# Feed-forward rotation: sine products on ScalarE tile by tile, output stores elsewhere; attention: V products of two key tiles in a row

## What is computed

```
x   = ln(src) * (1 + scale) + shift          # scale, shift from the step's embedding
q, k, v = x Wq + bq, x Wk + bk, x Wv + bv
p   = softmax(q k^T / sqrt(32) + attention_bias, masked)
x   = x + (p v) Wo + bo
h   = ln(x) * g2 + beta2
y   = x + gelu2(h W1 + b1) W2 + b2           # gelu2(u) = u * sigmoid(1.702 u)
# rotation, for each group of four columns of y, angles theta, phi of the batch
out = (y0 ct + y1 st, -y0 st + y1 ct, y2 cp + y3 sp, -y2 sp + y3 cp)
```

## Time and profile before

| | |
|---|---|
| median of 3 runs | 3400.22 us (3399.85 to 3401.56) |
| the profiled execution | 3405.53 us, its span 3403.7 us |
| PE busy | 3227.8 us (95%) |
| POOL busy | 2219.2 us (65%) |
| DVE busy | 2162.2 us (64%) |
| ACT busy | 1758.6 us (52%) |
| granted TensorE clock, mean | 0.986 |

### The profile page before, as it was taken

One profiled execution on the slowest core, in us unless ns is written; L12 is line 12 of the kernel. 1 busy time (PEld: TensorE's weight loads), 2 busy tenths in 40 slices (PEclk: granted clock), 3 DMA queues, 4 the chain that ended last, 5 costly groups with the idle time before them and its releaser, 6 DMA issues.

```text
span 3403.7 us, 52439 instructions
## 1 busy us (share of the span) xinstructions
PE 3227.8 (95%) x16592; PEld 2377.2 (70%) x16592; DVE 2162.2 (64%) x4445; ACT 1758.6 (52%) x3785; POOL 2219.2 (65%) x1503
## 2 busy tenths in 40 slices
PE   5999999999999999999969999999999999999997
PEld 4676776766776776776547677686877768677685
DVE  3777777777777777777667554545545455454542
ACT  2777777777777777777734232332323323232331
POOL 3788888888887888887546653555445454553525
PEclk9999999999999999999989999999999999999998
DMA  5998998989899988898666576574757658576563
GB/s 187 257 271 254 254 272 263 264 255 260 252 271 263 266 266 254 257 266 251 194 208 247 189 249 202 196 252 161 247 182 241 210 168 258 168 249 202 180 204 136
DMA packets 440432, 785.15 MB, mean 231 GB/s; under 512 B 57024, under 2 KB 106176, under 8 KB 440160
## 3 DMA queue, kind: packets, MB, share of 16 engines
q1 hardware_dynamic: 440160, 781.82, 75.1%
HBM read 591.76 MB, written 89.19 MB: 200 GB/s over the span
## 4 chain that ended last, share of the span: by engine, by line
PE 43%; DMA 2%; issue 2%; DVE 1%; POOL 1%; SPq 1%; ACT 0%; POOLq 0%; DVEq 0%; ACTq 0%
PE ps_out L1394 19%; PE ps_first L1374 18%; PE ps_first L1415 6%; DMA w_ring<-w_parts 2%; PE ps_first L1427 1%; DVE w_ring L1733 1%; POOL turned_out L1654 0%; DMA tmp<-context_t 0%; DVE turned_out L1773 0%; POOL turned_out L1653 0%; ACT g_hi L1491 0%; POOL y_b L1641 0%; SPq L1163 0%; DMA turned_out<-in_L_cond_W_dram 0%; DVE h_lo L1795 0%
## 5 line engine op out<-in xcount | busy, mean ns | idle before, releaser
L676 POOL TENSOR_TENSOR biasm<-biasm,maskb 128x1024 f32<-128x1024 f32 x512 | 1091.5, 2148 | 255.6 <-DMA biasm<-in_fside_Bx16xSxS_dram 252.7
L1394 PE MATMUL ps_out<-w_ring,g_hi 128*128 128x512 f32 x2048 | 691.4, 403 | 52.9 <-issue 39.2
L1374 PE MATMUL ps_first<-h_hi,w_ring 128*128 128x512 f32 x1792 | 558.9, 393 | 18.5 <-DVE tmp L1846 10.1
L1593 POOL TENSOR_TENSOR g_lo<-g_now,g_hi 128x512 fp32r<-128x512 f32 x128 | 168.4, 1316 | 539.0 <-ACT g_hi L1491 539.0
L1394 PEld LDWEIGHTS ps_out<-w_ring,g_hi 128*128 128x128 f32 x2048 | 391.2, 191 | 154.0 <-issue 67.4
L783 PE MATMUL ps_score<-k_rows,q_rows 96*128 96x512 f32 x1024 | 494.7, 483 | 3.6 <-issue 3.3
L923 DVE CUSTOM_DVE_ANT_0 prob_first<-ps_score,biasm 128x512 f32<-128x512 f32 x512 | 347.2, 686 | 214.1 <-PE ps_score L783 175.1
L834 ACT ACTIVATE probT<-ps_probT 128x512 f32<-128x512 f32 x512 | 304.6, 595 | 255.3 <-PE ps_probT L796 251.1
L923 DVE CUSTOM_DVE_ANT_0 prob_last<-ps_score,biasm 128x512 f32<-128x512 f32 x512 | 346.8, 686 | 122.7 <-PE ps_score L783 111.7
L850 ACT ACTIVATE prob_first<-prob_first,negmax 128x512 f32<-128x512 f32 x512 | 365.2, 716 | 91.0 <-DVE negmax L923 90.0
L796 PE MATMUL ps_probT<-ident,prob_first 128*128 128x128 f32 x2048 | 393.0, 273 | 16.3 <-DVE probT L501 13.7
(11 more groups left out here) (159 smaller groups left out, 5650.0 us busy)
## 6 DMA issues: line engine op xcount, KB each, us to landing
biasm<-in_fside_Bx16xSxS_dram SPq DMA_DIRECT2D x512, 512.0 KB, 5.4
w_ring<-w_parts SPq DMA_DIRECT2D x240, 512.0 KB, 3.6
w_ring<-w_parts SPq DMA_DIRECT2D x392, 256.0 KB, 3.5
k_rows<-k_hi SPq DMA_DIRECT2D x512, 64.0 KB, 4.8
q_rows<-q_hi SPq DMA_DIRECT2D x512, 64.0 KB, 3.3
xn<-in_x_dram SPq DMA_DIRECT2D x16, 1024.0 KB, 7.1
normal_rows<-xn SPq DMA_DIRECT2D x16, 1024.0 KB, 7.7
k_rows<-k_lo SPq DMA_DIRECT2D x256, 64.0 KB, 4.5
```

The costliest lines, as they stand in the source:

```text
L676: pool.tensor_tensor(tile, tile, maskb[:, 2 * half:2 * half + 2, :], ALU.add).then_inc(masked.sem, 1)
L1374: mm = pe.matmul(ps[:, BANK[n], :], w1r[:, place, w, cols], h[:, n, c, :], start=(c == 0 and k == 0 and not onto), stop=(c == 1 and k == 2 ...
L1394: mm = pe.matmul(ps_out[:, t, :], a[:, k % 2, cols], w2r[:, k % VR, w, :], start=(m == 0 and n == 0), stop=(m == NF - 1 and n == 2))
L1593: pool.tensor_tensor(GLO[:, k % 2, :], src, GHI[:, k % 2, :].bitcast(F32), ALU.subtract).then_inc(glo_done.sem, 1)
```

## The change

- Attention: V products of key tiles i and i + 1 both stand in the even slot i of the group's first head; the odd slots have none. The waits of each key tile come with it.
- `cross` moves from GpSimd to ACT, with `activation(Copy, scale=column)` in place of `tensor_scalar`. For e = 0 it stands behind `split_g` 4, 5, 8 and 9, one tile each; for e = 1 in steps 1 to 4 of the next pair, behind the last tanh and ahead of `split_g`. At the end of the run four in a row.
- `store_out` of e = 0 moves to m = 4, 5, 8 and 9 in SP's queue, one each, and `load_ysum` from m = 6 to m = 9. For e = 1 `rotate` and `store_out` come one step later (steps 2 to 5), `load_ysum` in step 6.
- The four totals of e = 1 move from between `u2` and `u3` of step 0 to behind the last gelu of that step. The list of rotations of e = 0 on DVE is written in another way and gives the same order.

```diff
--- before.py
+++ after.py
@@ -751,20 +751,18 @@
                 for j, i in slots(mode):
                     g, h = j // GH, j % GH
                     before = group_before(mode, b, g)
-                    if before is not None and h == 0:
-
-
+                    for kt in ((i, i + 1) if before is not None and h == 0 and i % 2 == 0 else ()):
                         pb, pg = before
-                        ((outT_act if i % 2 == 0 else outT_dve)
-                         .wait(pe, pb, 2 * (GH * pg + GH - 1) + i // 2))
+                        ((outT_act if kt % 2 == 0 else outT_dve)
+                         .wait(pe, pb, 2 * (GH * pg + GH - 1) + kt // 2))
                         if pg == 0:
-                            v_done.wait(pe, *v_event(pb, i))
-                        if i == 0:
+                            v_done.wait(pe, *v_event(pb, kt))
+                        if kt == 0:
                             ctx_done.wait(pe, b - 1 if g == 0 else b, NG - 1 if g == 0 else g - 1)
                         for hh in range(GH):
                             head = GH * pg + hh
-                            mm = pe.matmul(ps_ctx[HD * hh:HD * (hh + 1), 0, :], V[:, (NT * pb + i) % VR, HD * head:HD * (head + 1)],
-                                           probT[:, hh, i, :], start=(i == 0), stop=(i == NT - 1),
+                            mm = pe.matmul(ps_ctx[HD * hh:HD * (hh + 1), 0, :], V[:, (NT * pb + kt) % VR, HD * head:HD * (head + 1)],
+                                           probT[:, hh, kt, :], start=(kt == 0), stop=(kt == NT - 1),
                                            skip_group_check=True)
                         mm.then_inc(pv_done.sem, 1)
                     t = score_tile(mode, b, j, i)
@@ -1286,9 +1284,9 @@
                         load_rows(p + 1, 0)
                         for t in range(NT):
                             load_ctx(p + 1, 0, t)
-                    if 1 <= s <= NT and p > 0:
-                        store_out(p - 1, 1, s - 1)
-                    if s == NT + 1 and p > 0:
+                    if 2 <= s <= NT + 1 and p > 0:
+                        store_out(p - 1, 1, s - 2)
+                    if s == NT + 2 and p > 0:
                         load_ysum(p, 0)
                     if s == (NT if p else NT + 1) and ahead:
                         load_rows(p + 1, 1)
@@ -1318,11 +1316,14 @@
                     if ahead and m in (1, 2):
                         store_y(p + 1, NT + 2 * (m - 1))
                         store_y(p + 1, NT + 2 * (m - 1) + 1)
-                    if m in (4, 5):
-                        store_out(p, 0, 2 * (m - 4))
-                        store_out(p, 0, 2 * (m - 4) + 1)
-                    if m == 6:
-                        load_ysum(p, 1)
+                    if m in (4, 5, 8):
+                        store_out(p, 0, (4, 5, 8).index(m))
+                    if m == 9:
+                        finish_first(p)
+
+            def finish_first(p):
+                store_out(p, 0, NT - 1)
+                load_ysum(p, 1)
 
             start()
             for p in range(NP):
@@ -1525,6 +1526,19 @@
                     t_done.wait(act, q, T_OF[k - 6])
                 act.activation(HH[:, n, c, :], hf_of(e, cc), ACT.Copy).then_inc(hh_done.sem, 1)
 
+            def cross(p, e, t):
+                b = 2 * p + e
+                sum_done.wait(act, p, NT * e + t)
+                j = NT * e + t
+                out_done[t % 2].wait(act, p if j >= 2 else p - 1, j // 2 - 1 if j >= 2 else NT - 1)
+                rotated.wait(act, p if j >= 2 else p - 1, j - 2 if j >= 2 else 2 * NT - 2 + j)
+                y = ysum[:, t, :].rearrange("p (q r) -> p q r", r=4)
+                o = turned_out[:, t % 2, :, :]
+                for n in range(2):
+                    act.activation(o[:, :, 2 * n], y[:, :, 2 * n + 1], ACT.Copy, scale=rot[:, n, b:b + 1])
+                    mm = act.activation(o[:, :, 2 * n + 1], y[:, :, 2 * n], ACT.Copy, scale=rot[:, 4 + n, b:b + 1])
+                mm.then_inc(crossed.sem, 1)
+
             for e in range(2):
                 for i in range(NC):
                     take_columns(0, e, i)
@@ -1565,9 +1579,13 @@
                     tanh(p, s, 1, I_U3)
                     tanh(p, s, 2, I_C21)
                     tanh(p, s, 3, I_C12)
+                    if p > 0 and 1 <= s <= NT:
+                        cross(p - 1, 1, s - 1)
                     split_g(p, 0, 2 * s + 1)
                 for m in range(NF):
                     split_g(p, 1, m)
+                    if m in (4, 5, 8, 9):
+                        cross(p, 0, (4, 5, 8, 9).index(m))
                     if ahead and m in (5, 6):
                         take_columns(p + 1, 0, 2 * (m - 5))
                         take_columns(p + 1, 0, 2 * (m - 5) + 1)
@@ -1583,6 +1601,8 @@
                     if ahead and m in (11, 12, 13, 14):
                         split_columns(p + 1, 6 + 2 * (m - 11))
                         split_columns(p + 1, 7 + 2 * (m - 11))
+            for t in range(NT):
+                cross(NP - 1, 1, t)
 
         @block.gpsimd
         def _(pool):
@@ -1640,20 +1660,6 @@
                         pool.wait_ge(y_out[j % 2], y_out_at(q, j) - 16)
                 pool.tensor_tensor(to, yr[:, e, t, :], b2_rows[:, :], ALU.add).then_inc(y2_done.sem, 1)
 
-            def cross(p, e, t):
-                b = 2 * p + e
-                sum_done.wait(pool, p, NT * e + t)
-                j = NT * e + t
-                out_done[t % 2].wait(pool, p if j >= 2 else p - 1, j // 2 - 1 if j >= 2 else NT - 1)
-                rotated.wait(pool, p if j >= 2 else p - 1, j - 2 if j >= 2 else 2 * NT - 2 + j)
-                y = ysum[:, t, :].rearrange("p (q r) -> p q r", r=4)
-                o = turned_out[:, t % 2, :, :]
-                pool.sem_inc(pool_waited, 1)
-                for n in range(2):
-                    pool.tensor_scalar(o[:, :, 2 * n], y[:, :, 2 * n + 1], rot[:, n, b:b + 1], None, ALU.mult)
-                    mm = pool.tensor_scalar(o[:, :, 2 * n + 1], y[:, :, 2 * n], rot[:, 4 + n, b:b + 1], None, ALU.mult)
-                mm.then_inc(crossed.sem, 1)
-
             for j in range(NT):
                 modulate(0, j)
             power(0, 0)
@@ -1666,8 +1672,6 @@
             for p in range(NP):
                 ahead = p + 1 < NP
                 for s in range(NS):
-                    if p > 0 and 1 <= s <= NT:
-                        cross(p - 1, 1, s - 1)
                     if p == 0 and s + 1 < NS:
                         if s == 0:
 
@@ -1693,16 +1697,11 @@
                     power(p + 1, 3)
                 for m in range(2, NF):
                     split_g(p, 1, m)
-                    if m in (5, 7):
-                        cross(p, 0, m - 5)
-                        cross(p, 0, m - 4)
                     if ahead and m == 2:
                         power(p + 1, NT)
                         power(p + 1, NT + 1)
                     if ahead and m in (3, 4):
                         power(p + 1, NT + m - 1)
-            for t in range(NT):
-                cross(NP - 1, 1, t)
 
         @block.vector
         def _(dve):
@@ -1825,9 +1824,6 @@
                     dve.tensor_tensor(tmp[:, I_U2, :], ps[:, Y, :], tmp[:, I_P1, :], ALU.add).then_inc(u2_done.sem, 1)
                     if p == 0 and s + 1 < NS:
                         make_w1(s + 1, range(3))
-                    if p > 0 and s == 0:
-                        for t in range(NT):
-                            total(p - 1, 1, t)
                     prod.wait(dve, p, NW * s + N_S3)
                     u2_done.wait(dve, p, s)
                     if s == 0:
@@ -1838,8 +1834,8 @@
                     gelu(p, s, 0, I_C11)
                     if p == 0 and s + 1 < NS:
                         make_w1(s + 1, range(3, NW))
-                    if p > 0 and 1 <= s <= NT:
-                        rotate(p - 1, 1, s - 1)
+                    if p > 0 and 2 <= s <= NT + 1:
+                        rotate(p - 1, 1, s - 2)
                     f = s + NS
                     prod.wait(dve, p, NW * s + N_S1)
                     u3_done.wait(dve, p, s)
@@ -1854,6 +1850,9 @@
                         .then_inc(c12_done.sem, 1)
                     gelu(p, s, 2, I_C21)
                     gelu(p, s, 3, I_C12)
+                    if p > 0 and s == 0:
+                        for t in range(NT):
+                            total(p - 1, 1, t)
                 if ahead:
                     add(p + 1, 0)
                     add(p + 1, 1)
@@ -1875,11 +1874,12 @@
                     add(p + 1, NT + 3)
                     normalize(p + 1, NT + 2)
                     normalize(p + 1, NT + 3)
-                for t in range(NT):
+                for t in range(NT - 1):
                     rotate(p, 0, t)
                     if ahead and t == 1:
                         for k in range(4):
                             split_columns(p + 1, k)
```

(1 more changed line is left out.)

## The result

The changed kernel takes 3345.63 us (median of 4 runs, 3340.82 to 3351.45) against 3400.89 of the kernel before: ratio 0.9834, interval 0.9821 to 0.9846, some 55 us less. Forecast were 3327 and 73 us less. Time lies in the range (3300 to 3357), the direction is right, and the gain is three quarters of what was worked out.

A forecast was written before the change was run, and what follows sets the result against it. TensorE was taken as the bound in attention; in feed-forward second halves it waited for GpSimd's g_lo and others. 23.3 + 7 x 6.0 - 2.1 - 5.6 + 10.1 + 5.0 = 72.7 us saved: forecast 3327, range 3300 to 3357.

The forecast's parts named there:

- Price of a V product: Attention on TensorE: 1.19 us alone, of which 0.335 for leaving and entering; pairing saves 0.67 per group of four.
- Slot 32: Attention: the second V pair delays the transpose of x and its chain by 0.5 us, 7.5 us lost over 15 batches.
- Slots 0, 16 and 48: Attention: V groups there are followed by work that waits for nothing, so 46 groups save 0.67 each, 30.8 us.
- The clock: Feed-forward pairs: the one long wait before m = 12 may bring half clock; 0.8 us a pair, 5.6 lost.
- Cross on ACT: Feed-forward: four operations of 0.31 us, 1.25 a tile, fit ACT's queue under a limit of 1.97 without TensorE waiting.
- The tail: End of the run, after TensorE: faster cross lets the last rotation start earlier, 5.0 us gained.
- GpSimd's two waits: Second half of a pair, before m = 6 and 8: TensorE's waits for g_lo go, 6.0 us gained per pair.
- the wait before m = 12: Second half of a pair: ACT's split_g stands behind a split awaiting DVE's combine; about 3 us remain in one piece.
- The last pair: Its twelve products from 3331.98: 10.1 us of waits for cross and for loads behind stores, all gained.
- SP: Feed-forward: moved stores free the w2 loads and remove the load wait at m = 11; nothing counted for it.
- Late loads: Rival, attention: full DMA engines make mask additions wait for bias loads, the 30.8 us are lost: 3358; chance 0.16.
- The strided rival: Rival, feed-forward: ACT's strided cross costs what GpSimd's does, 2.9 us a tile, 22 us in all: 3352; chance 0.10.

The follow-up runs named there:

- single products: The changed kernel with the four V products at slots 32 to 35 one per slot again, other groups in pairs: 3333.6 us, ratio 0.9791.
- the stores alone: The kernel before with only the four stores and the ysum load of the second half at their new places in SP's queue: 3412.4 us, ratio 1.0026.

## Why the prediction was right, and where it was wrong

- **Price of a V product: right.** 1.86 for a pair (1.85 forecast); 0.59 and 0.65 per group against 0.67.
- **Slot 32: right.** -0.54 against -0.5, by the place named, and undone by single products.
- **Slots 0, 16 and 48 "are followed by work that waits for nothing": the step that failed.** It holds for two. The group at slot 48 gave 0.13, not 0.67, 14 x 0.54 = 7.6 of the 12 us missed in attention: four slots shorter by 0.67 left DVE, with the statistics of x in its queue, no room for its copy (with the statistics behind slot 52 the wait is gone). I had read DVE's mean share (153 of 200 us) where its queue in those slots was needed. In the one batch without statistics the interval is 24.48, the whole 0.67.
- **The clock: near in size by luck, wrong in place.** 5.6 were set for the seven pairs; two fell, 4.5, and in the other traces with the same wait none or one. That the clock "did not fall" behind the wait at m = 8 holds for the pair that was read, and not for the one at 2780. But in attention, where I had none, it fell in three batches, 4.2 us, behind the grown wait that I had forecast ("grown to about 2"; it is 0.58 and 1.27) without asking what it does to the clock.
- **Cross on ACT: mechanism right, size off.** 1.67 for 1.25, since the step of four costs 0.12 an operation; under the limit, so no wait. The tail gave 4.7 for 5.0.
- **GpSimd's two waits, the wait before m = 12, the totals: right.** 5.9 a pair for 6.0 less 0.3; 2.77 for about 3; 0.21 for 0.3. But DVE's chain alone was not what held m = 12: with ACT's splits one product later the wait is 0.83, before m = 13.
- **The last pair: right in size, misread.** 10.1 for 10.1, but the prediction called all of it waits; 6.4 were, and the clock and the new starts made the rest.
- **SP: right** that clearing its queue is worth nothing. The fall of the clock behind the merged wait, which the prediction did count (0.8 a pair), makes it a loss where the GpSimd waits stay; my 3400 for the stores alone had left it out.
- **Rivals.** Late loads did not decide this kernel, but batches made long by waits for transfers go from none to two a trace to five or six once attention is another 0.5 us a batch faster. The strided rival of 2.9 a tile is out at 1.67; its price was, if anything, low, as 2.4 a tile already cost 23 us.
- **From the profiled run to the median.** 5.3 us taken off that the changed kernel's own profiled run did not have; with runs up to 11 us apart in the changed kernel and 14 in the one before, that step adds its own error.

## What to carry to other kernels

Read the other engines' queues in the very slots that get shorter, not their mean share: a group whose successor waits for nothing today may wait for a copy once four slots are 0.67 us shorter. Before removing a wait or merging several, look at what the clock does behind waits of that length; a long one in one piece can cost more than two short ones (205.2 us a pair against 203.7). And put an operation that waits behind, not ahead of, the one that the bound engine needs next: moving eight such operations gave 23 us (17 of them found in the traces), where emptying SP's queue gave none.

## What the runs showed of the hardware

- ACT, 128 columns with a scale from a column: 0.29 us from start to start when contiguous, 0.415 with a step of four words in source and destination. From 64 and 128 columns with the step (0.30, 0.415) that is 1.8 ns a column, against 0.88 from the earlier trace rows.
- The granted clock fell to 1.2 GHz behind a wait of 1.27 us in attention in one to six of 15 batches of each kernel that had it, about 1.4 us each time, and behind none of the waits of 0.88 that stood there in the others.
- In the pairs: one wait of 2.77 alone, falls in two of seven (none or one in the other kernels that had it); waits of 2.74, 1.24 and 2.77, falls in all seven behind the first and the last; 1.31 and 1.65 with one product of 3.0 us between them, none. The length of the one wait doesn't decide it. What does was not settled.
